# Second cross-attention of a two-layer decoder: the next round's scores placed first in TensorE's round, projections and small turnings placed elsewhere

## The reference

```python
x = _layernorm(x + _L1_xattn_ref(ctx_1024, ctx_1024, x, mask_Bx1xSxS2_bk0, ...))

k = (key @ Wk.T + bk).reshape(bs, n_k, H, DK).transpose(0, 2, 1, 3)      # H = 16, DK = 16
q = (query @ Wq.T + bq).reshape(bs, n_q, H, DK).transpose(0, 2, 1, 3)
v = (value @ Wv.T + bv).reshape(bs, n_k, H, DK).transpose(0, 2, 1, 3)
scores = jnp.where(mask, jnp.einsum('bhmd,bhnd->bhmn', q, k), -1e10)
attn = jax.nn.softmax(scores / jnp.sqrt(DK), axis=3)
out = jnp.einsum('bhmn,bhnv->bhmv', attn, v).transpose(0, 2, 1, 3).reshape(bs, n_q, EDIM)
return out @ Wo.T + bo
```

## Time and profile before

| | before |
|---|---|
| median of 3 runs, us | 841.51 (840.01 to 844.86) |
| profiled execution, us | 838.83 |
| its span, first to last instruction, us | 837.0 |
| granted TensorE clock, mean | 0.997 |
| busy over the span: TensorE matmuls | 788.8 us (94%) |
| TensorE weight loads | 594.6 us (71%) |
| VectorE | 652.8 us (78%) |
| ScalarE | 610.5 us (73%) |
| GpSimdE | 426.4 us (51%) |

### The profile page before, as it was taken

How to read it: one execution, slowest core, us unless ns; L and a number is a source line. 1 busy time by engine, 2 the same in 40 slices (tenths; PEclk the granted TensorE clock), 3 DMA queues, 4 the chain that set the end, 5 groups by cost and what they waited for, 6 DMA issues and landing times.

```text
span 837.0 us, 20931 instructions
## 1 busy us (share of the span) xinstructions
PE 788.8 (94%) x6901; PEld 594.6 (71%) x6901; DVE 652.8 (78%) x2466; ACT 610.5 (73%) x1595; POOL 426.4 (51%) x459
## 2 busy tenths in 40 slices
PE   8998999999899988999999999999999999999996
PEld 7876777677667766767777777777666777676785
DVE  4997778889898767778778666785888888976667
ACT  4547977887885366887788877884999999984331
POOL 1264566666744145452554534224865666335763
PEclk9999999999999999999999999999999999999998
DMA  9301771122102458979869888875122212100001
GB/s 317 141 26 45 217 194 61 52 71 83 71 14 83 170 174 260 298 221 283 251 214 273 244 254 270 260 217 181 43 67 69 67 68 68 65 2 0 27 26 52
DMA packets 105393, 115.05 MB, mean 137 GB/s; under 512 B 29061, under 2 KB 94085, under 8 KB 105030
## 3 DMA queue, kind: packets, MB, share of 16 engines
q1 hardware_dynamic: 104724, 113.35, 42.8%
q10 hardware_dynamic: 562, 0.35, 0.1%
HBM read 48.09 MB, written 51.82 MB: 119 GB/s over the span
## 4 chain that ended last, share of the span: by engine, by line
PE 44%; ACT 7%; DVE 7%; issue 3%; DMA 3%; POOL 1%; SPq 0%; DVEq 0%; ACTq 0%
PE bank L1544 7%; PE bank L242 6%; PE bank L250 5%; PE bank L2267 4%; PE bank L2253 3%; PE bank L1559 3%; PE bank L2284 3%; PE bank L1528 2%; PE bank L1585 2%; PE bank L1595 2%; PE bank L2319 2%; ACT Sx L1750 2%; PE bank L234 1%; DMA skew_scratch<-rw 1%; ACT q_heads L1758 1%
## 5 line engine op out<-in xcount | busy, mean ns | idle before, releaser
L242 PE MATMUL bank<-x_feat,w_all_mats 128*128 128x256 f32 x384 | 92.4, 385 | 2.2 <-ACT q_full L358 0.6
L2997 POOL TENSOR_TENSOR bnd<-bnd,consts 128x60 f32<-128x60 f32 x64 | 18.1, 304 | 137.2 <-DMA bnd<-band_scratch 137.2
L242 PEld LDWEIGHTS bank<-x_feat,w_all_mats 128*128 128x128 f32 x384 | 70.4, 191 | 14.7 <-ACT rw L2644 3.8
L2602 ACT ACTIVATE bias_area<-bias_area,mq_two 128x256 f32<-128x256 f32 x128 | 66.5, 534 | 0.0
L1003 DVE COPY q_heads<-bank 128x512 f32<-128x512 f32 x64 | 42.0, 685 | 23.4 <-PE bank L717 23.3
L2778 DVE COPY q_heads<-bank 128x512 f32<-128x512 f32 x64 | 41.1, 683 | 22.8 <-PE bank L2267 22.8
L896 ACT ACTIVATE Sx<-Sx,mq 128x256 f32<-128x256 f32 x128 | 54.4, 497 | 5.4 <-DVE mq L995 5.4
L904 ACT ACTIVATE q_heads<-bank 128x512 f32<-128x512 f32 x64 | 37.7, 589 | 26.4 <-PE bank L717 26.4
L1750 ACT ACTIVATE Sx<-Sx,mq 128x256 f32<-128x256 f32 x128 | 54.3, 501 | 2.3 <-DVE mq L1848 2.3
L1856 DVE COPY q_heads<-bank 128x512 f32<-128x512 f32 x64 | 42.1, 685 | 17.0 <-PE bank L1544 17.0
L896 ACT ACTIVATE Pr<-Pr,mq 128x256 f32<-128x256 f32 x128 | 54.3, 501 | 0.9 <-DVE mq L995 0.9
(11 more groups left out here) (309 smaller groups left out, 2340.3 us busy)
## 6 DMA issues: line engine op xcount, KB each, us to landing
dist<-skew_scratch SPq DMA_DIRECT2D x64, 296.0 KB, 4.1
skew_scratch<-rw SPq DMA_DIRECT2D x30, 588.0 KB, 4.4
bnd<-band_scratch SPq DMA_DIRECT2D x64, 108.0 KB, 2.7
band_scratch<-bias_area SPq DMA_DIRECT2D x32, 162.0 KB, 3.2
band_scratch<-bias_area SPq DMA_DIRECT2D x32, 148.0 KB, 2.6
skew_scratch<-dist SPq DMA_DIRECT2D x4, 1024.0 KB, 7.7
context_values<-dist SPq DMA_DIRECT2D x8, 512.0 KB, 2.6
v_two<-context_values SPq DMA_DIRECT2D x8, 512.0 KB, 4.2
```

Of the source, the lines that this page charges most:

```text
L242: last = pe.matmul(dst[:, m * S:(m + 1) * S], w[:, k, m * P:(m + 1) * P], rhs[:, k, :], start=(k == 0), stop=(k == FT - 1))
L2602: last = act.activation(rows_of(n, g)[:, t, :], rows_of(n, g)[:, t, :], ACT.Exp, bias=mq_two[:, n % 2, g, t:t + 1], scale=-1.0, accum_out= ...
```

## The change

The order of TensorE's, ScalarE's and VectorE's lists in `attention_mask` changes; no instruction is added or taken away but waits.

- TensorE: `scores(pe, n + 1)` is the first work of each round, ahead of `turn(n, 0)`, in all four kinds of rounds. `x1_project_q` moves from the end of the third round (for batch b + 2) to the middle of the first round (for batch b + 1), between the turnings of heads 1 and 2. `project_rows` of the fourth round moves to the same place there. The transposing of `x_tok` in the second round moves behind `turn(n, 1)`, the second `turn_back` in the third round ahead of `turn(n, 0)`, the transposing of `at` stays between the turnings of heads 1 and 2.
- VectorE: part 0 of `norm_begin` moves ahead of the peaks of head 2 in the first round, parts 1 and 2 from the second round to the end of the first round's peaks. Both `normalise` stand behind all peaks of the third round. In the last batch the whole norm stands ahead of the fourth round's copies.
- ScalarE: `copy_ot` comes ahead of the query copy and `turn_x`; the query copy moves from the fourth round to the first, behind the exponentials.

```diff
--- before.py
+++ after.py
@@ -1608,9 +1608,15 @@
 
                 def first_round(b, n):
 
+                    scores(pe, n + 1)
                     turn(n, 0)
                     turn(n, 1)
-                    scores(pe, n + 1)
+                    if b >= 1 and b < B - 1:
+                        if b >= 2:
+                            pe.wait_ge(y_steps, 4 * (b - 2) + 1)
+                        else:
+                            pe.wait_ge(sa_xt_sb, B)
+                        x1_project_q(pe, b + 1, m_bank)
                     turn(n, 2)
                     turn(n, 3)
                     if b == 0:
@@ -1621,14 +1627,16 @@
 
                 def second_round(b, n):
 
+                    scores(pe, n + 1)
                     turn(n, 0)
-                    if b >= 2:
-                        pe.wait_ge(y_steps, 4 * (b - 2) + 1)
+                    turn(n, 1)
                     if b >= 3:
+                        if b < B - 1:
+                            pe.wait_ge(q_sb, b + 2)
+                        else:
+                            pe.wait_ge(y_steps, 4 * (b - 2) + 1)
                         pe.wait_ge(kept, b - 2)
                         transpose_tiles(pe, m_bank, x_tok[:, b - 3, :, :], xt_mm)
-                    turn(n, 1)
-                    scores(pe, n + 1)
                     turn(n, 2)
                     turn(n, 3)
                     if b == 0:
@@ -1638,51 +1646,43 @@
                     if b >= 1:
                         if b >= 3:
                             pe.wait_ge(xt_sb, b - 2)
-                        if b == 1:
-                            pe.wait_ge(q_sb, 3)
+                        else:
+                            pe.wait_ge(q_sb, b + 2)
                         pe.wait_ge(ot_sb, NQ * b)
                         turn_back(b - 1, 0)
                     weigh(n - 1)
 
                 def third_round(b, n):
 
-                    turn(n, 0)
+                    scores(pe, n + 1)
                     if b >= 1:
                         pe.wait_ge(normed, TT * (b - 1) + 1)
                         turn_back(b - 1, 1)
+                    turn(n, 0)
                     turn(n, 1)
-                    scores(pe, n + 1)
                     if b >= 1:
                         pe.wait_ge(normed, TT * b)
                         transpose_tiles(pe, m_bank, at, at_mm)
                     turn(n, 2)
                     turn(n, 3)
-                    if b < B - 2:
-                        if b >= 1:
-                            pe.wait_ge(at_sb, b)
-                        else:
-                            pe.wait_ge(sa_xt_sb, B)
-                        x1_project_q(pe, b + 2, m_bank)
-                    weigh(n - 1)
                     if b == B - 1:
                         pe.wait_ge(at_sb, b)
                         project_rows(pe, m_bank, aT, wo, y_mm)
+                    weigh(n - 1)
 
                 def fourth_round(b, n):
 
+                    if b < B - 1:
+                        scores(pe, n + 1)
                     turn(n, 0)
                     turn(n, 1)
-                    if b < B - 1:
-                        scores(pe, n + 1)
-                    else:
+                    if 1 <= b < B - 1:
+                        pe.wait_ge(at_sb, b)
+                        project_rows(pe, m_bank, aT, wo, y_mm)
+                    if b == B - 1:
                         gate_up(0)
                     turn(n, 2)
                     turn(n, 3)
-                    if 1 <= b < B - 1:
-                        pe.wait_ge(at_sb, b)
-                        if b < B - 2:
-                            pe.wait_ge(q_sb, b + 3)
-                        project_rows(pe, m_bank, aT, wo, y_mm)
                     weigh(n - 1)
                     if b == B - 1:
                         pe.wait_ge(y_steps, 4 * (B - 2) + 1)
@@ -1791,16 +1791,16 @@
                             act.wait_ge(sa_xt_mm, B)
                             act.activation(batch(x_feat, B - 1), m_bank[:, :].rearrange("p (f t) -> p f t", f=FT),
                                            ACT.Copy).then_inc(sa_xt_sb, 1)
-                        if j == 3 and b < B - 2:
-                            x1_copy_q(act, b + 2, m_bank)
                         if n >= 1:
                             turned(n - 1, 3)
                         exps(n, 2)
                         exps(n, 3)
+                        if n >= 2:
+                            copy_ot(n - 2)
+                        if j == 0 and 1 <= b < B - 1:
+                            x1_copy_q(act, b + 1, m_bank)
                         if j == 1 and b >= 3:
                             turn_x(b - 3)
-                        if n >= 2:
-                            copy_ot(n - 2)
                         if j == 2 and b >= 1:
                             turn_at(b - 1)
 
@@ -1880,18 +1880,20 @@
                         n = NQ * b + j
                         peaks(n, 0)
                         peaks(n, 1)
-                        if j == 2 and b >= 1:
-                            normalise(b - 1, 0)
-                        peaks(n, 2)
-                        peaks(n, 3)
                         if j == 0 and b >= 2:
                             dve.wait_ge(biased, b - 1)
                             if b == 2:
                                 dve.wait_ge(sa_kept, B)
                             ge(dve, kept, b - 2)
                             norm_begin(dve, y_steps, b - 2, y_mm, b - 1, m_bank, True, parts=(0,))
-                        if j == 1 and b >= 2:
-                            norm_begin(dve, y_steps, b - 2, y_mm, b - 1, m_bank, True, parts=(1,))
+                        peaks(n, 2)
+                        peaks(n, 3)
+                        if j == 0 and b >= 2:
+                            norm_begin(dve, y_steps, b - 2, y_mm, b - 1, m_bank, True, parts=(1, 2))
+                        if j == 3 and b == B - 1:
+                            dve.wait_ge(biased, b)
+                            dve.wait_ge(kept, b - 1)
+                            norm_begin(dve, y_steps, b - 1, y_mm, b, m_bank, True)
                         if n == 0:
                             dve.wait_ge(sa_biased, B)
                             dve.wait_ge(sa_kept, B - 1)
@@ -1899,14 +1901,9 @@
                         if n == 1:
                             keep_late(dve, KV_LATE)
                         if j == 2 and b >= 1:
+                            normalise(b - 1, 0)
                             normalise(b - 1, 1)
                         turned(n, 0)
-                        if j == 1 and b >= 2:
-                            norm_begin(dve, y_steps, b - 2, y_mm, b - 1, m_bank, True, parts=(2,))
-                        if j == 3 and b == B - 1:
-                            dve.wait_ge(biased, b)
-                            dve.wait_ge(kept, b - 1)
-                            norm_begin(dve, y_steps, b - 1, y_mm, b, m_bank, True, parts=(0,))
                         turned(n, 1)
 
                 def hidden(n):
@@ -1960,7 +1957,6 @@
                                                  rstd_two[i][:, tt:tt + 1], ALU.subtract, ALU.mult)
                     last.then_inc(xn_ready, 1)
 
-                norm_begin(dve, y_steps, B - 2, y_mm, B - 1, m_bank, True, parts=(1, 2))
                 hidden(0)
                 for n in range(1, NG):
                     hidden(n)
```

## The result

| | before | after |
|---|---|---|
| median, us | 841.5 (840.01 to 844.86) | 859.19 (858.25 to 859.74) |
| profiled execution, its span, us | 838.83, 837.0 | 858.8, 857.0 |
| granted TensorE clock, mean | 0.997 | 0.996 |
| busy: TensorE, VectorE, ScalarE, us | 788.8, 652.8, 610.5 | 790.7, 654.3, 610.9 |

The changed kernel takes 1.022 times as long, 95% interval 1.0199 to 1.0241 (the two medians of the table divide to 1.021): 859.19 against a forecast of 859.5 (851 to 867). Every engine does the same work as before; TensorE's share falls from 94% to 92% because the span grew.

The account below looks back on a forecast made before the run. Hand-overs among three nearly full engines bound the kernel; the change closes a 5.53 us loop per round. Losses of 3.4 (to S(9)), 13.0 (next five batches) and 3.1 (batch 7) sum to +19.5 on 838.83; predicted 859.5 (851 to 867).

Parts of the forecast that it names:

- The loop: Every round: peaks end, next scores, first turning, VectorE's two copies, next peaks; claimed 5.53 us a round.
- S: TensorE's next scores, at the head of each round; wait for all eight peak passes, then take 0.67 us.
- T0: First of a round's four turnings on TensorE; 0.70 us from its start to VectorE's first copy.
- The residual part: Norm step part 0 on VectorE, moved between the first round's peaks: one 128x512 pass, +0.60 us.
- third round's normalising: Both normalisings behind the third round's peaks: a 2.30 us chain against 1.57 for scores and first turning, +0.73.
- K2: Third head's peak passes on VectorE, first round: start at 4.13 instead of 3.95 us, +0.18.
- C1: Second of VectorE's two copies in a round; 0.09 us late in the second round, +0.08.
- signal term: In every round, from the last peak pass on VectorE to the scores on TensorE: taken as 0.20 us.
- B: Rival: nothing moves, waits merely change places and TensorE stays busiest; 840 us, chance 0.02.
- C: Rival: split queries and keys come late for the fourth round's scores, paid in six batches; 868 us, chance 0.06.
- D: Rival: TensorE's waits of about 1 us each round lower its clock; above 950 us, chance 0.01.
- A: Rival: TensorE becomes the limit, the round closes up, a batch falls toward 19.8 us; 829 us, chance 0.03.

Follow-up runs that it names:

- S first alone: The kernel before with one edit: the next scores stand first in every round, everything else at its old place; 870.65 us, ratio 1.038.
- S behind T0: The changed kernel with the next scores between the first two turnings in the first, second and fourth rounds; 848.52 us, ratio 1.014.
- half copies: The changed kernel with VectorE's two copies out of the turning banks cut to half their columns from the third round on; 849.38 us, ratio 1.012.
- one pass alone: The kernel before with only the first of the two score passes in batches 1 to 7; 837.86 us, ratio 0.998.

## Why the prediction was right, point by point

**The loop.** Shown: its waits stand in the trace where they were named (but for S of the second round, at which TensorE arrives with no idle time left), S first alone produces it, S behind T0 shortens it by the terms that leave it, and half copies shorten it by another. Its size was 0.06 too large, in one term: from the start of the last read-out of the peaks to S it takes 0.14 (660.70 to 660.84), not 0.20; 5.47 measured for 5.53., which counts from the same point, had 0.24. That ScalarE's row says 0.14 too is chance: it counts from the end of a copy, and from the end of the read-out to S it is 0.06.

**The additions, fourth to third round.** The residual part cost 0.59 (6.06 against 5.47; +0.60 said), the third round's normalising 0.70 (+0.73 said). Both rows were read rightly.

**First round: the mechanism was right, the size too large.** 5.71 was forecast, 0.18 over the loop, since the third head's peaks K2 must wait for T2 behind the projection; 5.50 came, 0.03 over it. T2 starts 3.34 after S (658.68 against 655.34) for a forecast 3.44 (whose terms add up to 3.42), and K2 0.64 after T2 for 0.69, so K2 is hardly late. That this wait is there shows once VectorE is earlier. In after with half copies the round stays at 5.50, and VectorE's timeline has the idle time ahead of K2:

```profile
655.54 0.08 DVE L1848 DVE_READ_ACCUMULATOR2_ANT mq<- 128x1 f32 x1
655.99 0.43 DVE L1848 CUSTOM_DVE_ANT_0 Pr<-bank,bias_area 128x256 f32<-128x256 f32 x1 [0.37 <-PE bank L1544]
```

**Second round: the mechanism was right, the size too small.** 5.61 was forecast, 5.74 came, 0.27 over a plain round for a forecast 0.08. T1 waits 0.25 for ScalarE; C1 then starts 0.88 after C0 (662.21 to 663.09), where two copies back to back end 1.20 after the first starts; here 1.48. The errors of these two rounds are one. T1 comes 7.08 after the first round's S (662.42 - 655.34), for a forecast 7.06: ScalarE's path through the query copy was read rightly. When the first round is shorter by 0.21, S and T0 of the second are ready earlier, and the wait for ScalarE grows by as much. From that T1 it is 0.67 to C1, 0.60 to the peaks, 2.76 through them and 0.14 to S: 666.59, and S came at 666.58. So these two rounds together are set by ScalarE's path, with VectorE's behind it, and not by the loop alone.

**The sum.** The rows at which the stage's parts begin in after, answering to the earlier trace rows, from TensorE's timeline: first scores of the stage, S(9), S(29), T0 of the last round.

```profile
583.54 1.89 PE L242 MATMUL bank<-x_feat,w_all_mats 128*128 128x256 f32 x8
585.36 1.15 PE L1525 MATMUL bank<-c_feat,q_par 32*128 32x256 f32 x16
...
631.88 0.74 PE L1528 MATMUL bank<-x_k_cells,x_q_cells 32*128 32x256 f32 x16 [0.69 <-DVE mq L1848]
...
749.22 0.74 PE L1528 MATMUL bank<-x_k_cells,x_q_cells 32*128 32x256 f32 x16 [0.69 <-DVE mq L1848]
...
766.95 1.09 PE L1544 MATMUL bank<-ident,Sx 128*128 128x128 f32 x8
```

The projection ahead of the stage (583.54) began 2.07 later than in the profiled execution of before (581.47), and the change touches nothing ahead of it. Over the executions profiled here that instruction begins anywhere from 579.8 to 586.6, so this part is not the change's. From there, S(9) is later by 2.95 (3.4 said; its own terms give 3.34), S(9) to S(29) by 11.92 (117.34 against 105.42; 13.0 said), S(29) to T0 of the last round by 2.95 (17.73 against 14.78; 3.1 said), and the rest of the span by 0.11. Together 17.9, where the sum was 19.5: 1.6 too much, which is the signal term in some 27 rounds, while the errors of the first and second round (-0.21 and +0.13 a batch, the signal's 0.06 in each) nearly cancel, for the reason just given. The medians differ by 17.7. That 859.5 came so near 859.19 is partly luck of the basis: it stood between the profiled execution and the median, and 841.5 + 17.9 = 859.4 would have been the right way to it.

**The rivals.** B (nothing moves) fell with the waits above. C (queries and keys late) did not occur: the fourth round's S, as at 672.75, is ended by VectorE's peaks and by no DMA. (The first two terms of that chain, 3.54 and 6.7, add up to 10.2, not 10.4, which leaves a little more slack than was said.) D did not occur: the granted clock stayed at 1.00 (2.4 GHz) in every round, with waits of up to 1.03. A did not occur either, and came as near as its margin of 0.2 had said: in the first round TensorE is busy 5.37 of 5.50.

## What to carry to other kernels

When three engines stand near their limit, write out for each instruction you move the closed loops that go through it, with each hand-over from a row (here 0.14 from the end of a copy to TensorE, 0.70 from the start of a turning to its copy), and take the longest loop of each round; busy shares don't tell. An instruction that looks like a cost on the busiest engine may fill the gap in which two shared buffers change hands, and then taking it away, or shortening it, wins little until the copy behind it gets shorter too (here 0.14 a batch, and 0.64 with the copies halved). Try the parts of a change apart: here each part alone was as slow as the whole or slower, which no sum of parts would have told.

## What the runs showed that was not expected

- Two PSUM banks that serve four turnings in turn make a loop of at least 1.53 us per bank (turning, 0.70 to the copy, copy, signal back), seen as waits of 0.33 to 0.44 in the kernels in which S has left the gap or is shorter; of the 0.67 us of scores in that gap, 0.24 taken out in each round won 0.14 in a whole batch.
- Two copies of 128x512 end 1.20 after the first starts when they run back to back, but 1.48 after it when the second waits 0.19: the short wait cost more than its length.
- The instruction with which the stage begins moved by up to 6.8 us (579.8 to 586.6) between executions of kernels that are the same up to there, so a difference of two spans needs the entry of the changed stage taken off. The latest entry is that of S first alone, whose profiled execution took 873.86, 3.2 above its median.
- What bounds the second round of the kernel before (4.90 in every variant of it whose scores stand behind T1 there, but for 4.98 with one pass alone) was not tried apart; its T1 waits for ScalarE. No run beat the kernel before with all of its work done.
